# Perceiver cross attention on one Trainium2 core: mixing four chunks at a time, and moving the split of K from ScalarE and VectorE to VectorE and GpSimd

## The reference, cut to what matters

```python
Q = (x @ Wq + bq).reshape(256, 16, 32)
K = (ctx @ Wk + bk).reshape(25088, 16, 32)
V = (ctx @ Wv + bv).reshape(25088, 16, 32)
scores = einsum('bihd,bjhd->bijh', Q, K) / sqrt(32)
attn = softmax(scores, axis=1)      # over the 256 queries i, for each context row j
x = einsum('bijh,bjhd->bihd', attn, V).reshape(256, 512) @ Wo + bo
```

## Time and profile before

| what | value |
|---|---|
| median of 3 runs | 2783.01 us (2781.40 to 2783.21) |
| the profiled execution, its own time | 2780.41 us |
| its span | 2778.3 us, mean granted clock 0.986 |
| busy, share of the span | PE 97%, ACT 72%, DVE 71%, POOL 30% |
| chain that ended last | PE 85%, DVE 5%, POOL 5% |

### The profile page before, as it was taken

One profiled execution on the slowest core, in us unless ns is written; L12 is line 12 of the kernel. 1 busy time (PEld: TensorE's weight loads), 2 busy tenths in 40 slices (PEclk: granted clock), 3 DMA queues, 4 the chain that ended last, 5 costly groups with the idle time before them and its releaser, 6 DMA issues.

```text
span 2778.3 us, 58556 instructions
## 1 busy us (share of the span) xinstructions
PE 2687.2 (97%) x21096; PEld 2197.9 (79%) x21096; DVE 1964.5 (71%) x3791; ACT 2009.9 (72%) x7210; POOL 838.7 (30%) x1144
## 2 busy tenths in 40 slices
PE   7998899999999999999999999999999997899998
PEld 5775899877787787777778778777877875699997
DVE  6775776577777777777777777777777776555555
ACT  2112444299999999999999999999999995345553
POOL 4431211133333333333333333333333322122222
PEclk9999999999999999999999999999999998999999
DMA  9983454556666655666566666566666653345451
GB/s 344 393 313 156 162 201 172 145 146 158 150 156 161 160 150 151 156 160 160 149 159 152 151 168 155 152 152 157 155 160 155 158 123 114 152 180 192 183 182 69
DMA packets 132291, 473.26 MB, mean 170 GB/s; under 512 B 31128, under 2 KB 31256, under 8 KB 124832
## 3 DMA queue, kind: packets, MB, share of 16 engines
q1 hardware_dynamic: 132000, 469.52, 57.9%
HBM read 244.47 MB, written 17.30 MB: 94 GB/s over the span
## 4 chain that ended last, share of the span: by engine, by line
PE 85%; DVE 5%; POOL 5%; DMA 2%; issue 2%; ACT 1%; SPq 0%; POOLq 0%
PE PB L573 19%; PE PB L598 14%; PE PB L606 12%; PE PB L586 11%; PE PB L672 6%; PE PB L687 6%; PE PB L535 5%; PE PB L403 5%; POOL CTX L1424 3%; PE PB L548 3%; DVE small L1183 2%; POOL VS L1435 1%; DVE V L1179 1%; PE PB L431 1%; PE PB L462 1%
## 5 line engine op out<-in xcount | busy, mean ns | idle before, releaser
L815 ACT ACTIVATE EE<-PB,small 128x256 f32<-128x256 f32 x3136 | 1446.0, 482 | 133.2 <-DVE small L1183 119.9
L1183 DVE TENSOR_REDUCE small<-PB 128x2 f32<-128x512 f32 x1568 | 1062.0, 678 | 440.3 <-PE PB L598 439.7
L1435 POOL TENSOR_TENSOR VS<-V,small 128x128 f32<-128x128 f32 x784 | 348.5, 444 | 1206.7 <-DVE small L1189 1206.7
L815 ACT ACTIVATION_READ_ACCUMULATOR EE<-PB,small 128x1 f32 x3136 | 663.3, 212 | 0.0
L598 PEld LDWEIGHTS PB<-QS,STK 128*128 128x128 f32 x3136 | 480.5, 190 | 204.2 <-issue 165.3
L573 PE MATMUL PB<-CTX,WKV 128*128 128x256 f32 x4704 | 624.7, 282 | 0.0
L598 PE MATMUL PB<-QS,STK 128*128 128x256 f32 x3136 | 605.6, 295 | 8.0 <-issue 4.8
L573 PEld LDWEIGHTS PB<-CTX,WKV 128*128 128x128 f32 x4704 | 588.9, 190 | 0.1
L606 PE MATMUL PB<-EE,VS 128*32 128x256 f32 x6272 | 426.6, 386 | 8.4 <-POOL VS L1435 8.4
L586 PE MATMUL PB<-WKV,CTX 128*128 128x512 f32 x1584 | 432.5, 395 | 0.8 <-DVE V L1179 0.8
L586 PEld LDWEIGHTS PB<-WKV,CTX 128*128 128x128 f32 x1584 | 273.0, 190 | 36.9 <-DVE V L1179 1.2
(11 more groups left out here) (198 smaller groups left out, 2494.9 us busy)
## 6 DMA issues: line engine op xcount, KB each, us to landing
STK<-KHL SPq DMA_DIRECT2D x1568, 128.0 KB, 2.8
RW<-in_l1f SPq DMA_DIRECT2D x32, 2048.0 KB, 8.1
AR<-in_ctx SPq DMA_DIRECT2D x49, 1024.0 KB, 8.2
RAW<-in_ctx SPq DMA_DIRECT2D x98, 512.0 KB, 4.2
WF<-in_l0f SPq DMA_DIRECT2D x17, 2304.0 KB, 8.8
v_scr<-RAW SPq DMA_DIRECT2D x64, 256.0 KB, 8.2
V<-v_scr SPq DMA_DIRECT2D x64, 256.0 KB, 2.9
WA<-in_l0a SPq DMA_DIRECT2D x1, 4096.0 KB, 12.4
```

The source lines that it names most:

```text
L815: m = e.activation(EE[:, b, s, :], bank(2 * (k % 2) + half, 256 * (s % 2), 256), ACT.Exp, bias=nm[:, b, s:s + 1], accum_out=su[:, b, s:s + 1])
L1183: e.tensor_reduce(nm[:, k % 4, 2 * half:2 * half + 2], bank(2 * (k % 2) + half).rearrange("p (s i) -> p s i", s=2), axis=AX.X, op=ALU.max, ...
L1435: e.tensor_tensor(VS[:, b, :].rearrange("p (s d) -> p s d", s=4), V[:, t % 4, 128 * c:128 * c + 128].rearrange("p (s d) -> p s d", s=4), r ...
```

## The change

- **Mix.** `MIX = 4`: at the end of every fourth chunk four mixes run, of chunks k-5 to k-2. VS, EE and the small maxima, sums and reciprocals have `RING = 6` places instead of 4. `exps(k)` waits for `mix(k-6)`.
- **K.** `k_hi` leaves ScalarE. VectorE's `k_raw` (the new L1184) copies bank 4 plus the bias to a new buffer KR (two places), behind both maxima and the reciprocals of the same chunk. GpSimd's `split_k` (new L1458 and L1460) makes hi (a copy with rounding) and lo (a subtraction) from KR, directly behind `scale_v` and ahead of `split_lo`. TensorE waits for `kr_out` before it projects K into bank 4 again, and `stack_k` waits for `kr_lo`.
- **VectorE's order.** Both maxima of a chunk stand together; the reciprocals now stand ahead of `v_out`.
- **WO.** QHL moves into other memory, so the load of WO (1 MB) is issued in chunk 40 of the loop instead of ahead of it.

```diff
@@ sync @@
-            e.dma_start(WO[:, :, :], ...)
...
             def stack_k(g):
-                w.wait_ge("k_lo", 4 * g + 4)
+                w.wait_ge(*k_done(g, 3))
...
+                if k == 40:
+                    w.wait_ge("d_q", 256)
+                    e.dma_start(WO[:, :, :], ...)
@@ tensor @@
                 scores(k, 0)
                 if due_k(k):
                     g, ch = due_k(k)
-                    w.wait_ge("k_lo", 4 * g + ch)
+                    if k:
+                        w.wait_ge("kr_out", 4 * (g - 2) + ch)
                     project_k(g, ch)
...
                 scores(k, 1)
-                if k % 2 and k >= 3:
-                    mix(k - 3)
-                    mix(k - 2)
+                if k % MIX == MIX - 1:
+                    for n in range(max(k - MIX - 1, 0), k - 1):
+                        mix(n)
@@ scalar @@
-                if k >= 4:
-                    w.wait_ge("mix_mm", k - 3)
+                if k >= RING:
+                    w.wait_ge("mix_mm", k - RING + 1)
...
                 exps(k, 0)
-                if due_k(k):
-                    k_hi(*due_k(k))
                 exps(k, 1)
@@ vector @@
+            def k_raw(g, ch):
+                n = 4 * (g - 2) + ch
+                w.wait_ge("kp_mm", 4 * g + ch + 1)
+                if n >= 2:
+                    w.wait_ge("kr_lo", n - 1)
+                e.tensor_scalar(KR[:, n % 2, :], bank(4, 0, GT), BC[:, C_L1XK + ch:C_L1XK + ch + 1], None,
+                                ALU.add).then_inc(S["kr_out"], 1)
...
                 maxima(k, 0)
-                if k and due_k(k - 1):
-                    k_lo(*due_k(k - 1))
                 maxima(k, 1)
+                if k >= 1:
+                    reciprocals(k - 1)
+                if due_k(k):
+                    k_raw(*due_k(k))
                 if due_v(k) and due_v(k)[1] == 2:
                     v_out(due_v(k)[0])
-                if k >= 1:
-                    reciprocals(k - 1)
@@ gpsimd @@
+            def split_k(g, ch):
+                n = 4 * (g - 2) + ch
+                w.wait_ge("kr_out", n + 1)
+                if ch == 0:
+                    w.wait_ge(f"d_s{g % 2}", 256 * (g // 2))
+                e.tensor_copy(KHL[:, g % 2, 0, ch, :], KR[:, n % 2, :]).then_inc(S["kr_hi"], 1)
+                w.wait_ge("kr_hi", n + 1)
+                e.tensor_tensor(KHL[:, g % 2, 1, ch, :], KR[:, n % 2, :], KHL[:, g % 2, 0, ch, :].bitcast(F32),
+                                ALU.subtract).then_inc(S["kr_lo"], 1)
...
                 if k >= 1:
                     scale_v(k - 1)
+                if k >= 1 and due_k(k - 1):
+                    split_k(*due_k(k - 1))
                 if k % 8 == 5 and k // 8 + 3 < NG:
                     split_lo(k // 8 + 3)
```

More of the change, by code:

```diff
@@ L31 @@
 NPC = 32
+MIX = 4
+RING = 6
 PASSES = ((0, 0), (0, 1), (1, 0))
@@ L43 @@
 f0_xs f0_xs_act f0_hi f0_lo f0_plo f0_up f0_silu f0_mul f0_hhi f0_hlo f0_dn f0_acc gate_mm gate_sig gate_comb
-ctx_hi ctx_lo kp_mm k_hi k_lo q_mm q_out q_split vp_mm v_out s_mm s_max s_exp s_rcp vs mix_mm ot_dve ot_act xo_mm x_xo x_xbias
+ctx_hi ctx_lo kp_mm k_hi k_lo kr_out kr_hi kr_lo q_mm q_out q_split vp_mm v_out s_mm s_max s_exp s_rcp vs mix_mm ot_dve ot_act xo_mm x_xo x_xbias
 f1_xs f1_xs_act f1_hi f1_lo f1_plo f1_up f1_gelu f1_hhi f1_hlo f1_dn f1_acc g1_mm g1_sub g1_exp g1_comb g1_turn g1_pt b2_mm b2_out f1_half x_lnb y_out
@@ L155, in build @@
         V = sb("V", [P, 4, D], over=life)
-        VS = sb("VS", [P, 4, P], over=life)
-        EE = sb("EE", [P, 4, 4, 256], over=life)
+        KR = sb("KR", [P, 2, GT], over=life)
+        VS = sb("VS", [P, RING, P], over=life)
+        EE = sb("EE", [P, RING, 4, 256], over=life)
         OT = sb("OT", [P, NC, 256], over=life)
+        q_life = ExitStack()
+        QHL = sb("QHL", [P, 2, NC, 256], F32R, q_life)
+        q_life.close()
         WO = sb("WO", [P, NC, D], over=life)
-        QHL = sb("QHL", [P, 2, NC, 256], F32R, life)
         life.close()
@@ L225, in build, with k_done @@
         qf = EE[:, 3].rearrange("p c i -> p (c i)")
-        nm = small[:, 0:16].rearrange("p (b s) -> p b s", b=4)
-        su = small[:, 16:32].rearrange("p (b s) -> p b s", b=4)
-        rc = small[:, 32:48].rearrange("p (b s) -> p b s", b=4)
+        nm, su, rc = (small[:, o:o + 4 * RING].rearrange("p (b s) -> p b s", b=RING) for o in (0, 32, 64))
         KBANK = ((6, 2, 3, 7), (6, 2, 3, 4))
+        def k_done(g, ch):
+            return ("k_lo", 4 * g + ch + 1) if g < 2 else ("kr_lo", 4 * (g - 2) + ch + 1)
         WS1 = (WSA, WSB)
@@ L311, in sync_program @@
             e.dma_start(wqx, a["l1x"][:, 0:2048].rearrange("p (c n) -> p c n", c=NC)).then_inc(S["d_wx"], 16)
-            e.dma_start(WO[:, :, :], a["l1x"][:, 2048:4096].rearrange("p (c n) -> p c n", c=NC)).then_inc(S["d_wo"], 16)
             def stack_k(g):
-                w.wait_ge("k_lo", 4 * g + 4)
+                w.wait_ge(*k_done(g, 3))
                 if g >= 2:
@@ L349, in sync_program @@
                     load_ctx(g + 6)
+                if k == 40:
+                    w.wait_ge("d_q", 256)
+                    e.dma_start(WO[:, :, :], a["l1x"][:, 2048:4096].rearrange("p (c n) -> p c n", c=NC)).then_inc(S["d_wo"], 16)
             def load_piece(n):
@@ L602, in mix @@
             def mix(k):
-                t, c, b = k // 4, k % 4, k % 4
+                t, c, b = k // 4, k % 4, k % RING
                 w.wait_ge("vs", k + 1)
@@ L803, in k_hi @@
                 w.wait_ge("kp_mm", 4 * g + ch + 1)
-                if g >= 2 and ch == 0:
-                    w.wait_ge(f"d_s{g % 2}", 256 * (g // 2))
                 e.activation(KHL[:, g % 2, 0, ch, :], bank(kb, 0, GT), ACT.Identity,
@@ L809, in exps @@
             def exps(k, half):
-                b = k % 4
+                b = k % RING
                 w.wait_ge("s_max", 2 * k + half + 1)
-                if k >= 4:
-                    w.wait_ge("mix_mm", k - 3)
+                if k >= RING:
+                    w.wait_ge("mix_mm", k - RING + 1)
                 for s in (2 * half, 2 * half + 1):
@@ L1183, in maxima @@
                 e.tensor_reduce(
-                    nm[:, k % 4, 2 * half:2 * half + 2], bank(2 * (k % 2) + half).rearrange("p (s i) -> p s i", s=2),
+                    nm[:, k % RING, 2 * half:2 * half + 2], bank(2 * (k % 2) + half).rearrange("p (s i) -> p s i", s=2),
                     axis=AX.X, op=ALU.max, negate=True).then_inc(S["s_max"], 1)
@@ L1188, in reciprocals @@
                 w.wait_ge("s_exp", 2 * k + 2)
-                e.reciprocal(rc[:, k % 4, :], su[:, k % 4, :]).then_inc(S["s_rcp"], 1)
+                e.reciprocal(rc[:, k % RING, :], su[:, k % RING, :]).then_inc(S["s_rcp"], 1)
             split_hi(0)
@@ L1428, in scale_v @@
             def scale_v(k):
-                b, t, c = k % 4, k // 4, k % 4
+                b, t, c = k % RING, k // 4, k % 4
                 w.wait_ge("s_rcp", k + 1)
```

## The result

The changed kernel takes 2824.61 us, the median of 4 runs (2821.53 to 2826.24), against 2782.48 us for the kernel before in the same comparison (4 runs, 2781.40 to 2783.21). The ratio is 1.015, with a 95% interval of 1.0133 to 1.0168. So it is slower by 42 us, where 54 were forecast.

What follows compares the result with a forecast made beforehand. TensorE's own instructions were taken to bound the kernel. Blocks -61, old wait -13 and new wait +128 gave +54 us, so 2783 + 54 = 2837 us, with a range of 2790 to 2886 for 8 in 10.

Steps and rivals of the forecast that it cites:

- The blocks: TensorE's mixes in half as many blocks: 191 blocks fewer at 0.32 us each, 61 us less.
- The new wait: mix(5) on TensorE waits 1.35 us for scale_v(5), queued on GpSimd behind split_k and split_lo, in 95 groups: 128 us more.
- The terms of `split_k`: On GpSimd: copy 0.40 us, wait for its own semaphore 0.10, subtraction 0.75, together 1.25 us.
- The old wait: TensorE's second mix waiting for scale_v(5) in every third group, where v_out comes ahead: 13 us, gone inside the new wait.
- What cost nothing: K off ScalarE, k_raw on VectorE, the later stack_k and the load of WO: each taken as 0.
- The late load of WO: Ahead of the first scores: taken as 0, with at most 3.4 us less as a bound.
- GpSimd was not fast enough to hide `split_k`: Rival, chance 0.10: GpSimd's work fits in front of mix(5), stall under 0.78 us, so faster, 2709 to 2775 us.
- contention did not grow to matter: Rival, chance 0.06: VectorE slows GpSimd, split_k takes 2.0 us, stall 2.1 us, +126 us, 2909 us.
- That the blocks save nothing: Rival, chance 0.04: the 0.32 us belongs to each mix or bank, not the block; +115 us, 2898 us.
- worth nothing: Taking k_hi off ScalarE in each even chunk: no gain, since ACT isn't waited for in the loop except at its end.

Runs made afterwards that it cites:

- older pairs: e8 with the mixes in pairs behind every odd chunk, of chunks k-5 and k-4, instead of blocks of four: 2766.11 us, ratio 0.9943.
- e12: The changed kernel with the K of chunk 4 split behind scale_v(5) instead of ahead of split_lo: 2731.98 us, ratio 0.9825.
- e8: The changed kernel with split_hi and split_lo of the context in chunk 3 of a group instead of chunk 5: 2704.07 us, ratio 0.9724.

## Why the prediction was right

**The blocks, -61 us: right.** Between the starts of the scores behind one block and the next the trace of the changed kernel has 8.69 us in the half of a group without the wait. Four chunks of before are two pairs of 4.51, 9.02 us, so the block that is gone was worth 0.33. The older pairs measured 62 us for all of them.

**The new wait, +128 us: the right place and count, a little too long.** The number of waits is 95, as worked out, and the size is 1.25 us instead of 1.35, so 119 us. The terms of `split_k`: the copy took 0.39 (taken 0.40), the subtraction started 0.08 after it (taken 0.10), and the next instruction started 0.69 after the subtraction's start though it takes 0.74. Together 1417.11 - 1415.95 = 1.16 us against 1.25. That a start comes ahead of the end before it could be read in the earlier trace rows, where it is 0.04 each time, and the working left it out for the inserted instructions. A mix is 0.43 and not 0.44. That the copy came out within 0.01 is partly luck: the 0.40 was chosen between a memset and an affine select, no row before had a copy on GpSimd, and the range allowed 0.32 to 0.75. With the wait at 1.25 us a group takes 18.6 us (18.7 forecast).

**The old wait, -13 us: gone,** as its place was taken by the new one. The sum with the measured wait is -61 - 13 + 119 = +45 us. The two profiled executions differ by 44.5 and the medians by 42, with runs that spread by 2 to 5 us.

**What cost nothing: right.** ScalarE's busy time fell by 152 us, and no wait for ScalarE in the loop was there to be shortened. `k_raw` took 0.45 us (`k_lo` took 0.48), and the reciprocals of chunk 4 came when expected. `kr_out` and the stacked K (`d_s`) don't show among TensorE's waits from 600 us on. The late load of WO gained nothing: the first scores behind the first block start at 554.32 us, before at 554.41.

**The rivals.** GpSimd was not fast enough to hide `split_k`, and contention did not grow to matter: the CAST meets one GpSimd instruction in a group as it did before, see the last section. That the blocks save nothing is refuted by the older pairs. What I didn't see is the other side of the K path: I put it at "worth nothing", since ScalarE wasn't waited for. For the mixes in pairs that fits the older pairs (2766 us, against 2781 less the old wait of 13), though no run has the old K path in pairs without that wait. But for blocks of four it is worth 88 us once the queue is in order, since `k_lo` behind the next chunk's maxima would have come too late. The sum was not touched, because both came together; a forecast of the blocks alone would have been wrong.

## What to carry to other kernels

Before moving work to the idle engine, look at what stands behind it in that engine's queue at its tightest place: POOL was busy 30% of the time, and 1.16 us in front of one `scale_v` out of eight made most of a wait that cost 119 us. Moving that one insertion out of the way (e12) gave 93 us back, while the three other insertions of a group cost nothing once the order was right (e8). The rest of the wait came with the blocks, which reach `mix(5)` 0.3 us sooner. When a stall has that form, reorder the queue before taking work off it; here two changed positions turned +42 us into -76 us with the same instructions. And ask of each of two edits what the other hides. Blocks of four without the new K path are 0.4 to 0.6% slower than before. The new K path without the blocks is 2.7 to 2.8% slower with GpSimd's queue in the way, and 0.6% faster with older pairs, which the queue can't hold; that is about the old wait. Together, in the right order, they give 2.8%. Whether moving the splits in the kernel before would have taken the old wait of 13 us away by itself was not run.

## What the runs showed of the hardware

```profile
L1448 POOL TENSOR_TENSOR VS<-V,small 128x128 f32<-128x128 f32 x784 | 332.0, 429 | 814.3 <-DVE small L1202 807.6
L1460 POOL TENSOR_TENSOR KHL<-KR,KHL 128x256 fp32r<-128x256 f32 x384 | 293.4, 764 | 30.7
L1437 POOL TENSOR_TENSOR CTX<-RAW,CTX 128x1024 fp32r<-128x1024 f32 x96 | 227.2, 2366 | 25.7 <-DVE CTX L1165 25.7
L1458 POOL CAST KHL<-KR 128x256 fp32r<-128x256 f32 x384 | 152.0, 396 | 0.0
```

These are GpSimd's groups of the changed kernel by shape (count, busy us, mean ns, idle before). A one-input rounding copy of 128x256 takes 0.39 us there and the two-input subtraction 0.73 to 0.74, so the copy costs half. I had no row for it. The slowing beside VectorE's CAST follows whatever GpSimd happens to run: `scale_v(4)` in most groups (0.76 for 0.40), and in the third of the groups where `v_out` puts the CAST later, the subtraction, which took 1.06 us 32 times and 0.74 us 352 times. In the kernel with the copy made twice it is, again 32 times, the second copy (1413.40):

```profile
1412.94 0.40 POOL L1458 CAST KHL<-KR 128x256 fp32r<-128x256 f32 x1
1413.40 0.74 POOL L1459 CAST KHL<-KR 128x256 fp32r<-128x256 f32 x1
1414.23 0.73 POOL L1461 TENSOR_TENSOR KHL<-KR,KHL 128x256 fp32r<-128x256 f32 x1
```

One meeting with the CAST costs GpSimd's instruction 0.32 to 0.36 us in each case. The CAST can be held up as well: in the changed kernel it takes 0.87 us instead of 0.66 in the groups where the subtraction meets it.
